# Second attention layer, batches 1 to 3: projections from rounded and rest halves, weights in pieces, projections ahead of the scores

## The reference

```python
q = _split_heads(jnp.einsum('bnd,df->bnf', x, Wq))        # 256 -> 16 heads x 64
kv = jnp.einsum('bmc,cf->bmf', context, Wkv)              # 512 -> 2 x 1024
k, v = jnp.split(kv, 2, axis=-1)
k, v = (_split_heads(k), _split_heads(v))
k = jnp.concatenate((nk, k), axis=-2)                     # one null key and value
v = jnp.concatenate((nv, v), axis=-2)
sim = jnp.einsum('bhid,bhjd->bhij', q * scale, k)
out = jnp.einsum('bhij,bhjd->bhid', jax.nn.softmax(sim, axis=-1), v)
out = jnp.einsum('bnf,fd->bnd', out.transpose(0, 2, 1, 3).reshape(b, -1, INNER), Wout)
```

## Time and profile before

| | us |
|---|---|
| median of 3 runs | 1825.76 (1825.55 to 1828.7) |
| the profiled execution | 1830.33 |
| its span, first to last instruction | 1828.6 |
| mean granted clock of TensorE in it | 0.983 |
| busy in the span: TensorE, VectorE, ScalarE, GpSimd | 1696.2, 1195.2, 1045.7, 375.5 |

### The profile page before, as it was taken

How to read it: one execution, slowest core, us unless ns; L and a number is a source line. 1 busy time by engine, 2 the same in 40 slices (tenths; PEclk the granted TensorE clock), 3 DMA queues, 4 the chain that set the end, 5 groups by cost and what they waited for, 6 DMA issues and landing times.

```text
span 1828.6 us, 27461 instructions
## 1 busy us (share of the span) xinstructions
PE 1696.2 (93%) x9294; PEld 1082.1 (59%) x9294; DVE 1195.2 (65%) x2830; ACT 1045.7 (57%) x2160; POOL 375.5 (21%) x374
## 2 busy tenths in 40 slices
PE   5899998899799899999999999999998888999998
PEld 3455555455455345444554455444645788999997
DVE  3867876876778667555567457664676688666632
ACT  2467666666666656655555546555455466666621
POOL 2101110120011010000000000200021467777721
PEclk9899999999999999999999999999999899999999
DMA  3000000010003009200000000100001757777775
GB/s 104 1 24 1 1 24 1 1 28 3 1 1 138 2 2 347 73 24 1 1 1 23 1 1 1 58 2 1 13 25 56 227 148 218 214 210 198 218 230 161
DMA packets 121147, 127.10 MB, mean 70 GB/s; under 512 B 9904, under 2 KB 116400, under 8 KB 121008
## 3 DMA queue, kind: packets, MB, share of 16 engines
q1 hardware_dynamic: 113280, 116.68, 20.2%
q0 software_dynamic: 7152, 8.66, 2.6%
q10 hardware_dynamic: 576, 0.00, 0.0%
HBM read 96.46 MB, written 29.77 MB: 69 GB/s over the span
## 4 chain that ended last, share of the span: by engine, by line
PE 53%; DVE 5%; DVEq 1%; issue 1%; SPq 1%; ACT 0%; DMA 0%; POOLq 0%
PE psum L2497 8%; PE psum L1845 6%; PE psum L1716 6%; PE psum L1700 6%; PE psum L1722 5%; PE psum L1831 5%; PE psum L2515 4%; PE psum L1707 3%; PE psum L2472 3%; PE psum L1756 2%; PE psum L2482 1%; DVE moe_w_lo L2615 1%; DVE l_k_lo L2109 1%; DVE l_k_hi L2107 1%; PE psum L2454 0%
## 5 line engine op out<-in xcount | busy, mean ns | idle before, releaser
L1273 DVE TENSOR_REDUCE l_tile_max<-psum 128x1 f32<-128x512 f32 x512 | 342.1, 689 | 109.9 <-PE psum L951 108.2
L1121 ACT ACTIVATE l_probs<-psum 128x1024 f32<-128x1024 f32 x256 | 248.3, 1022 | 105.7 <-PE psum L963 102.0
L951 PE MATMUL psum<-l_kT,l_qT 128*128 128x512 f32 x512 | 238.3, 473 | 40.1 <-DVE l_tile_max L1273 36.8
L2049 DVE TENSOR_REDUCE l_row_max<-psum 128x2 f32<-128x1024 f32 x124 | 151.6, 1223 | 140.7 <-PE psum L1700 139.9
L2784 POOL TENSOR_TENSOR moe_w_lo<-moe_w,moe_w_hi 128x512 fp32r<-128x512 f32 x128 | 179.9, 1407 | 92.7 <-ACT moe_w_hi L2568 91.6
L951 PEld LDWEIGHTS psum<-l_kT,l_qT 128*128 128x128 f32 x512 | 98.0, 192 | 132.3 <-DVE l_tile_max L1273 111.7
L1888 ACT ACTIVATE l_probs<-psum,l_neg_max 128x512 f32<-128x512 f32 x248 | 167.2, 674 | 0.0
L963 PE MATMUL psum<-l_qT,l_kT 128*128 128x512 f32 x512 | 160.4, 397 | 1.7 <-ACT l_probs L1121 1.5
L1831 PEld LDWEIGHTS psum<-ident,l_probs 128*128 128x128 f32 x1024 | 120.5, 143 | 68.8 <-issue 53.1
L2599 ACT ACTIVATE moe_gate<-psum 128x256 f32<-128x256 f32 (+1 forms) x184 | 64.7, 352 | 158.7 <-PE psum L2497 98.5
L2497 PE MATMUL psum<-moe_xs_hi,moe_w_hi 128*128 128x256 f32 x512 | 148.0, 289 | 1.4 <-DVE moe_xs_lo L2625 1.4
(11 more groups left out here) (361 smaller groups left out, 3278.6 us busy)
## 6 DMA issues: line engine op xcount, KB each, us to landing
moe_w<-in_moe_w SPq DMA_DIRECT2D x276, 256.0 KB, 4.6
moe_sorted_x<-l_null_cols SPq DMA_DIRECT2D x1, 17680.0 KB, 56.4
moe_xs<-moe_sorted_x SPq DMA_DIRECT2D x16, 272.0 KB, 2.9
moe_w<-in_ctx SPq DMA_DIRECT2D x8, 512.0 KB, 3.6
moe_w<-in_ctxT SPq DMA_DIRECT2D x4, 1024.0 KB, 5.7
moe_w<-in_wkv SPq DMA_DIRECT2D x2, 2048.0 KB, 15.7
x_resid<-in_x SPq DMA_DIRECT2D x4, 512.0 KB, 11.0
out_x<-x_resid SPq DMA_DIRECT2D x4, 512.0 KB, 4.4
```

Source lines behind the costliest of these rows:

```text
L951: nc.tensor.matmul(bank(max_bank(m)), qT[:, q % SLOTS, h, t * P:(t + 1) * P], kT[:, q % SLOTS, h // 2, half * BANK:(half + 1) * BANK], sta ...
L1121: nc.scalar.activation(probs[:, n % PT_RING], wide(2 * (n % 2)), ACT.Exp, scale=SCALE).then_inc(exp_done, 1)
L1273: nc.vector.reduce_max(tile_max[:, q % 2, t, h, half:half + 1], bank(max_bank(m)), AX_X).then_inc(max_read, 1)
L2049: nc.vector.reduce_max(row_max[:, t, :], wide(2 * (t % 2)).rearrange("p (j m) -> p j m", j=2), AX_X)
```

## The change

From batch 1 on (groups i of 8 and more) q, k, v and from batch 1 the null scores are made of three products of rounded numbers (type fp32r) in place of one f32 product: hi x hi, hi x lo and lo x hi, where hi is the rounded number and lo what is left. That needs hi and lo of both operands:

- xT: ScalarE rounds a fill into `xT_hi`, VectorE subtracts into `xT_lo`.
- The weights are no longer kept whole. SP loads them in f32 by pair of heads (wq 2 x 128 columns, wk 4 x 128, two buffers each) or by half of the heads (wv, 4 x 512, one buffer), the context in two halves; ScalarE rounds each piece (`round_*`), and VectorE subtracts in place (`split_*`). wk of group i + 2 is rounded in quarter 0, wq of group i + 3 in quarter 2, wv in p = 5, quarters 2 and 3, four pieces, and in p = 2, one piece a quarter, the context in p = 6, quarters 0 and 1.
- The rest halves of the null keys' weights are made once, in batch 0.

In all groups, those of batch 0 too, TensorE makes q ahead of the scores in quarter 0, and the second half of k ahead of them in quarter 2; VectorE reads q and k out of bank 7 ahead of the maximum.

```diff
     def is_split(fill):
-        return fill[0] in ("q", "k") and fill[1] >= 2
+        return fill[0] in ("q", "k") and fill[1] >= 2 or fill[0] == "xT" and fill[1] >= 1
...
+        WK, WQ, HALF, ALL = s.CC * P, s.DC * P, s.CC * s.I1, s.CC * BANK
+        wk_raw = w13_flat[:, 0:2 * WK].rearrange("p (i c n) -> p i c n", i=2, c=s.CC)
+        wk_lo = place("l1_wk_lo", [P, 2, s.CC, P], F32R, "w13")
+        wk_hi = place("l1_wk_hi", [P, 2, s.CC, P], F32R, "w13", 2 * WK)
+        ctx_hi = place("l1_ctx_hi", [P, s.CC, s.M], F32R, "w13", 4 * WK)
+        wv_raw = w13_flat[:, HALF:HALF + ALL].rearrange("p (c n) -> p c n", c=s.CC)
+        wv_lo = place("l1_wv_lo", [P, s.CC, BANK], F32R, "w13", HALF)
+        wv_hi = place("l1_wv_hi", [P, s.CC, BANK], F32R, "w13", HALF + ALL)
+        wq_raw = w2_flat[:, 0:2 * WQ].rearrange("p (i c n) -> p i c n", i=2, c=s.DC)
+        wq_lo = place("l1_wq_lo", [P, 2, s.DC, P], F32R, "w2")
+        wq_hi = place("l1_wq_hi", [P, 2, s.DC, P], F32R, "w2", 2 * WQ)
+        xT_lo = place("l1_xT_lo", [P, s.DC, N], F32R, "w2", 4 * WQ)
+        ctx_lo = place("l1_ctx_lo", [P, s.CC, s.M], F32R, "w2", s.DC * s.I1)
+        xT_hi = place("l1_xT_hi", [P, s.DC, N], F32R, "rows", T * D)
...
             @block.sync
             def _(sp):
+                def load_queries(i):
+                    cols = slice(i % PAIRS * P, (i % PAIRS + 1) * P)
...
+                sp.wait_ge(misc_psum, last_fill("v", 0, 1, KT - 1))
+                load_values(0)
+                for n in range(PAIRS - 1, GROUPS):
+                    b, p = divmod(n - 2, PAIRS)
+                    coming = (n + 1, n + 2) if n == PAIRS - 1 else (n + 2,) if n + 2 < GROUPS else ()
+                    sp.wait_ge(misc_psum, last_fill("q", n))
+                    for i in coming:
+                        load_queries(i)
+                    sp.wait_ge(misc_psum, last_fill("k", n))
+                    for i in coming:
+                        load_keys(i)
+                    if n % PAIRS == PAIRS - 1 and b + 1 < s.B:
+                        load_context(b + 1)
+                    if p == 0 and b >= 1:
+                        sp.wait_ge(misc_psum, last_fill("v", b, 0, KT - 1))
+                        load_values(1)
+                    if p == 3 and b >= 2:
+                        sp.wait_ge(residual_added, b - 1)
+                        sp.dma_start(out[b - 2].rearrange("(t p) n -> p t n", p=P), tokens(b - 2)).then_inc(g["base_stored"], 16)
+                    if p == 4 and 1 <= b and b + 1 < s.B:
+                        sp.wait_ge(misc_psum, last_fill("v", b, 1, KT - 1))
+                        load_values(0)
...
+                def product(out, weights, moving, first, stop):
+
+                    terms = ((0, 0), (0, 1), (1, 0))
+                    for n, (x, y) in enumerate(terms):
+                        last = nc.tensor.matmul(out, weights[x], moving[y], start=(first and n == 0),
+                                                stop=(stop and n == len(terms) - 1))
+                    return last
...
                 def project_queries(i):
                     p = i % PAIRS
+                    if i >= PAIRS:
+                        pe.wait_ge(wq_split, i - PAIRS + 1)
                     for c in range(s.DC):
-                        last = nc.tensor.matmul(bank(MISC), wq[:, c, p * P:(p + 1) * P], xT[:, c, :],
-                                                start=(c == 0), stop=(c == s.DC - 1))
+                        first, stop = c == 0, c == s.DC - 1
+                        if i >= PAIRS:
+                            last = product(bank(MISC), (wq_hi[:, i % 2, c, :], wq_lo[:, i % 2, c, :]),
+                                           (xT_hi[:, c, :], xT_lo[:, c, :]), first, stop)
+                        else:
+                            last = nc.tensor.matmul(bank(MISC), wq[:, c, p * P:(p + 1) * P], xT[:, c, :], start=first, stop=stop)
                     return last
...
+                    if b >= 1 and chunks[0] == 0:
+                        pe.wait_ge(wk_split, i - PAIRS + 1)
+                    if b >= 1 and p == 0:
+                        pe.wait_ge(ctx_split, 2 * (b - 1) + (1 if chunks[0] == 0 else 2))
...
+                    if b >= 1 and kt == 0:
+                        pe.wait_ge(wv_split, s.CC * (2 * (b - 1) + half + 1))
...
                 for i in range(GROUPS):
                     for r in range(4):
+                        if r == 0:
+                            fill((i, r, 0))
+                        if r == 2 and i + 2 < GROUPS:
+                            project_keys(i + 2, range(s.CC // 2, s.CC)).then_inc(misc_psum, 1)
                         if i + 1 < GROUPS:
                             scores(i + 1, r)
-                        fill((i, r, 0))
-                        if r == 2 and i + 2 < GROUPS:
-                            project_keys(i + 2, range(s.CC // 2, s.CC)).then_inc(misc_psum, 1)
+                        if r != 0:
+                            fill((i, r, 0))
                         transpose_probs(i, r)
...
-                        last = nc.scalar.activation(xT[:, rest[1], :], bank(MISC), ACT.Copy)
+                        nc.scalar.activation(xT_hi[:, rest[1], :], bank(MISC), ACT.Copy).then_inc(xT_rounded, 1)
+                        return
...
+                def round_queries(i):
+                    act.wait_ge(wq_in[i % 2], 16 * ((i - PAIRS) // 2 + 1))
+                    nc.scalar.activation(wq_hi[:, i % 2], wq_raw[:, i % 2], ACT.Copy).then_inc(wq_rounded, 1)
+
+                def round_keys(i):
+                    act.wait_ge(wk_in[i % 2], 16 * ((i - PAIRS) // 2 + 1))
+                    nc.scalar.activation(wk_hi[:, i % 2], wk_raw[:, i % 2], ACT.Copy).then_inc(wk_rounded, 1)
+
+                def round_values(b, half, c):
+                    act.wait_ge(wv_in, 16 * (2 * (b - 1) + half + 1))
+                    nc.scalar.activation(wv_hi[:, c, :], wv_raw[:, c, :], ACT.Copy).then_inc(wv_rounded, 1)
+
+                def round_context(b, half):
+                    some = slice(half * s.CC // 2, (half + 1) * s.CC // 2)
+                    act.wait_ge(ctx_in[half], 16 * b)
+                    nc.scalar.activation(ctx_hi[:, some], ctxT[:, some], ACT.Copy).then_inc(ctx_rounded, 1)
+
+                def round_soon(i, r):
+                    b, p = divmod(i, PAIRS)
+                    if r == 0 and PAIRS <= i + 2 < GROUPS:
+                        round_keys(i + 2)
+                    if p == 6 and r < 2 and b + 1 < s.B:
+                        round_context(b + 1, r)
+
+                def round_later(i, r):
+                    b, p = divmod(i, PAIRS)
+                    if r == 2 and PAIRS <= i + 3 < GROUPS:
+                        round_queries(i + 3)
+                    if p == 5 and r >= 2 and b + 1 < s.B:
+                        for c in (2 * r - 4, 2 * r - 3):
+                            round_values(b + 1, 0, c)
+                    if p == 2 and b >= 1:
+                        round_values(b, 1, r)
...
                         read_fill((i, r, 0))
+                        round_soon(i, r)
                         if i + 1 < GROUPS:
                             exponentials(i + 1, r)
                         keep_probs(i, r)
                         read_fill((i, r, 1))
+                        round_later(i, r)
                         if r == 0 and i >= 1:
...
+                    elif kind == "xT":
+                        dve.wait_ge(xT_rounded, 2 * (rest[0] - 1) + rest[1] + 1)
+                        last = nc.vector.tensor_tensor(xT_lo[:, rest[1], :], bank(MISC), xT_hi[:, rest[1], :].bitcast(F32),
+                                                       ALU.subtract)
...
+                def split_queries(i):
+                    dve.wait_ge(wq_rounded, i - PAIRS + 1)
+                    nc.vector.tensor_tensor(wq_lo[:, i % 2], wq_raw[:, i % 2], wq_hi[:, i % 2].bitcast(F32),
+                                            ALU.subtract).then_inc(wq_split, 1)
...
+                def split_soon(i, r):
+                    b, p = divmod(i, PAIRS)
+                    if r == 0 and PAIRS <= i + 2 < GROUPS:
+                        split_keys(i + 2)
+                    if p == 6 and r < 2 and b + 1 < s.B:
+                        split_context(b + 1, r)
+
+                def split_later(i, r):
+                    b, p = divmod(i, PAIRS)
+                    if r == 2 and PAIRS <= i + 3 < GROUPS:
+                        split_queries(i + 3)
+                    if p == 5 and r >= 2 and b + 1 < s.B:
+                        for c in (2 * r - 4, 2 * r - 3):
+                            split_values(b + 1, 0, c)
+                    if p == 2 and b >= 1:
+                        split_values(b, 1, r)
...
                     for r in range(4):
-                        if i + 1 < GROUPS:
-                            maxima(i + 1, r)
                         if r == 0:
                             read_fill((i, 0, 0))
```

(9 more changed lines are left out.)

91 lines of the change are left out of this document (73 added, 18 removed).

## The result

| | before | after |
|---|---|---|
| median | 1827.21 (4 runs, 1825.55 to 1828.7) | 1854.47 (4 runs, 1853.03 to 1859.76) |
| profiled execution | 1830.33 | 1855.42 |
| its span | 1828.6 | 1853.7 |
| mean granted clock | 0.983 | 0.976 |

The ratio is 1.0155, with a 95% interval from 1.0131 to 1.0178: **slower by 28 us**. The forecast was slower by 7, so the sign was right and the size too small. 1854.5 lies in the stated range (1798 to 1858), but above the 1820 to 1847 that the forecast gave itself.

A forecast was written before the change was run, and what follows sets the result against it. TensorE's work was taken to bound the attention stage. Losses of 65 us against gains of 45 (products) and 13 (waits that go) made it 7 us slower, 1833 us beside the median of 1825.76; forecast 1820 to 1847, stated range 1798 to 1858.

The forecast's parts named there:

- rival B: Attention stage: waits of 3 to 5 us at two places of each batch lower the clock, 1851 us; chance 0.15.
- TensorE bounds, the other two have slack in their sums: Second layer's attention: stage as long as TensorE's work; after the change VectorE at 69%, ScalarE at 62%.
- Products, 45 us: Batches 1 to 3: three rounded products replace one f32; 72 halves gain 0.41 each, 24 value fills 0.64, 45 us.
- upper bound of 52: Products' gain if a rounded product is exactly half a step of the f32 one, 0.215 us: 52 us.
- reading of 0.10 for the change of type: After the scores' last pair on TensorE: 0.10 of the 0.33 us to the next work read as change of type.
- Quarter 1's wait, 0.63 in 21 groups: Quarter 1's transposes wait for quarter 0's late copy: 0.63 us in 21 groups, with batch 0's six 14 us.
- p = 0 and p = 2 of batch 0, 2.05 each and 0.2 elsewhere: Batch 0: 2.05 us lost at each of pairs 0 and 2, 4 us; f32 halves leave 0.2 in six groups.
- p = 5 into p = 6, 26 us: Pairs 5 and 6: second xT fill and k halves wait behind copy and subtractions, 9.3 us three times, 7.3 in batch 0.
- Router fills, 6 us: Router's transposes in quarters 2 and 3, three times: second fill waits for ScalarE's reading behind the copy, 6 us.
- A: Handoffs absorb the waits, perhaps 30 of the 65 us left: faster, 1798 us; chance 0.27.
- C: Weights late: ScalarE stops at a rounding with all exponentials behind it, 1833 + 12 = 1845 us; chance 0.06.
- D: Products no cheaper, since each one loads its weights anew: 1833 + 45 = 1878 us; chance 0.02.

The follow-up runs named there:

- x1: The changed kernel with the old order back on TensorE and VectorE (scores and maximum first), rounded products and weight pieces kept: 1825.30 us, ratio 0.9969.
- x2: The kernel before with the new order alone, products and weights still f32 and whole: 1856.55 us, ratio 1.0147.
- x3: The changed kernel, new order, with weight pieces made for their first use only (later projections wrong), context still split: 1846.43 us, ratio 1.0087.
- x9: x1 with the new order in quarter 0 only, on both engines: 1845.14 us, ratio 1.0106.
- x10: x1 with the new order in quarter 2 only, on both engines: 1840.85 us, ratio 1.0057.
- x4: The changed kernel in the old order, with weight pieces made for their first use only (later projections wrong), context still split: 1813.74 us, ratio 0.9923.
- x11: x1 with the new order only in quarter 2 of p = 5 and 6 (k's second half ahead, read ahead of the maximum): 1828.35 us, ratio 1.0001.

## Why the prediction was right in sign and short in size

The order as a cost larger than the products' gain was foreseen, and x1 and x2 show it. The size was missed by 21 of 28 us. That it was not missed by more is in part luck: too large a gain of the products and nothing for four of the router's groups stand on one side of the sum, too large a loss in quarter 1 and at p = 5 and 6 on the other. And 1854.5 is nearer to rival B's 1851 than to the forecast's 1833, without B's mechanism being the main one.

**TensorE bounds, the other two have slack in their sums**: right. VectorE was busy 64% and ScalarE 58% of the stretch, and dropping most of the pieces gave only 8 to 12 us (x3).

**Products, 45 us**: too high. In the old order a half gives 0.33 where 0.41 was forecast, and the 24 v fills about 16 us, 39.5 in all. (Rounded products are 0.23 apart and an f32 one costs 0.86, 3.7 times as much and not four times, so the upper bound of 52 was out of reach.) The step that failed is the reading of 0.10 for the change of type. It is the change of shape with its uncovered load, and it is paid on both sides: in x1 the scores' last pair is followed after 0.33, and the first product behind it after 0.34, where 0.23 is usual. The prediction counted one of the two. (Its 0.64 a v fill is also not the mean of its own 0.73 for the 9 first and 0.50 for the 15 second fills, which is 0.59.) **And the new order adds one such change in each of quarters 0 and 2**, 0.15 us each by x9 and x10, 9 us over 30 groups, which the prediction put at nothing. The products themselves gain in the new order what they gain in the old: q takes 1.58 us to the scores (1028.82 to 1030.40) against 1.92 in x2, 0.34 less. That a plain group is only 2.02 us shorter than x2's (22.37 against 24.39) and not 2.31 is the wait.

**Quarter 1's wait, 0.63 in 21 groups**: the chain was right to 0.0 us (copy at 7.20), its other side was not. In plain groups it is listed with 0.21 and costs 0.43; the mean of the 27 listed waits is 0.59. In the sum with the products this leaves 0.2 us a group, as shown above. x9 shows that the place was right: in a plain group quarter 0's order costs 0.57 of the 0.68 us of both (22.37 against x1's 21.69).

**p = 0 and p = 2 of batch 0, 2.05 each and 0.2 elsewhere**: 5.8 us measured, 5.0 forecast.

**p = 5 into p = 6, 26 us**: the size was about right (14.8 us net against 17.5), the cause half wrong. The second xT fill waits 2.70, 3.06, 2.71 us (forecast 2.8). The first k half waits 2.16, 1.68 and 2.00, and in two of the three batches q has waited 1.00 before it (forecast 5.2). But it is not the pieces that make it: without most of them 11.6 remain (x3), in the old order with them 15.5 (x1), with neither 8.8 (x4). The causes cover one another, and taking away one gives little. All four kernels make the halves of the context at p = 6, for which the first k half waits (5.9 us after the change, 4.9 in x3); leaving those out was not tried.

**Router fills, 6 us**: here the prediction failed. It looked at the router's fills in quarters 2 and 3 and passed over the four **second fills of quarter 0** (p = 0 and 3 of batches 2 and 3), whose reading stands behind the late copy or the late maximum with quarter 1's k half waiting for it. These four groups are 12.8 us over what the terms give them, nearly the whole miss of 14 in the stage. Their waits of 1.8 to 2.4 us, 8.3 together, are the larger part; each of the four also holds a spell of the lower clock behind its wait, 13.6 us together, which can cost up to half of that. The sixth line of the waits and half of the third (two k halves, 3.6 us) are theirs; the other half is quarter 3 of p = 7, which was forecast. They are slower in x2 too (25.00 at p = 0, 26.11 at p = 3, against 23.04 and 25.49), so it is the order. A smaller one of the kind is q, first of its quarter now, behind ScalarE's reading of v (5.3 us in seven waits).

**Rival B, the clock**: in part true. TensorE was granted the lower of its two levels for 13.7 us of the stage before and 37.5 after (x2 23.9, x1 27.3). Each of these costs at most half of itself, so at most 12 us more than before; it falls behind the new waits, as in the row at 1060 us. In the table it is counted with the places (it is part of the 12.8). By the Trainium skill (TensorE: Matmul & The Clock Gate, HAM oscillation) waits between bursts bring the clock down again and again; the trace agrees in part: there are more low spells with more waits, behind waits shorter than the prediction asked for, as the 1.82 us at 1061.35. But such a wait alone is not enough: x2 waits 1.83 us at the same place of batches 2 and 3 and keeps the full clock, and the changed kernel does so behind 1.91 at 1045.9.

**Rivals A, C, D**: the handoffs did not absorb it (58 us of waits); no engine waited for a weight; products are 0.23 apart at full clock, as in the earlier trace rows.

**The account.** Forecast -45 + 3 (null) - 13 + 62 (waits) = 7; for the profiled execution that makes 1837.3, not the 1837.5 that the prediction has. Measured in the stage: -39.5 + 3 + 9 (uncovered loads) + 38 (listed waits) = 10.5, and 21.8 in all. For the remaining 11 there are the lower clock, at most 12, and the part of each new wait that the list leaves out, some 0.2 as in the plain group. They were not measured apart: comparing each distance of TensorE's starts with the usual one of the same operations in the same trace gives the lower clock 7 to 10 us, an estimate. So the waits added were 11 us fewer than forecast, the products gave 5.5 less, and the loads and the clock, 9 and about 10, were at nothing in the sum. Another 3.3 us of the span lie outside: 4.4 from the last scores on, less 1.1 ahead of the stage. From the last scores on the other kernels have from 0.3 us less than before (x2) over 1.3 (x4) and 2.9 (x1) to 7.8 more (x11), with no pattern that the runs explain. What makes them was not tried.

The version that beats both kernels is x1, by 0.3% over before, with products, pieces and the old order.

## What to carry to other kernels

An order in which a fill comes "ready earlier" is paid on every chain behind it: before moving work ahead of the step that starts a chain (here scores, maximum, exponentials, copy), list every fill whose reading stands behind that chain's end, in all quarters, and not only in those that were edited. Try the new arithmetic and the new order apart: here the one gained 5 us and the other lost 26 to 34. And when several waits stand at one place, expect that removing any one of them gives much less than its size.

## What the runs showed of the hardware

- Where the shape of the weights changes between two matmuls (64*128, 128*64, 128*128), the first weight load is not ahead of its matmul: 884.55 and 884.55, 885.44 and 885.45, against 0.43 ahead within f32 work of 128*128 and 0.23 within rounded work. In x1 the distance into such a change is 0.33 instead of 0.23, the first one behind it 0.34; one change more made 0.16 us a quarter in x2.
- 24 matmuls of 16 columns take 2.7 us at full clock, 0.11 each. In batch 1 of x1 the clock was low behind them (0.66 from 1005 us), so that the weighing takes 1.9 instead of 1.0, in batch 2 from their start on, in batch 0 not at all.
- A wait of 1.8 us brought the clock down in the changed kernel (1061.35) and did not at the same place in x2 (1063.0). What decides it was not found.
- GpSimd at work in memory stretched some of VectorE's operations that read and write memory (485 to 567 ns, a sum of two columns from 167 to 210, but not the reciprocal, 166), not those from PSUM (1221).
- Half of an order is worse than either: one engine reading in another order than the one in which its source delivers cost 23 to 48 us.
